# Attention and mixture of experts on one core: the first norm and the parts shared over more engines, and 16-bit parts for the scores

## The reference

```
h   = layernorm(x)                                  # over the 128 channels
s   = (h * w_lhs) @ (h * w_rhs).T                   # per sequence, 1024 x 1024
x   = x + softmax(s) @ h
g   = layernorm(x)
p   = softmax(g @ router_w.T)                       # 8 experts, the best two kept and made to sum to 1
x   = x + sum over the two experts of  p_e * (gelu(g @ w_fc[e] + b_fc[e]) @ w_proj[e] + b_proj[e])
```

## Time and profile before

| what | us |
|---|---|
| median of three runs (306.63 to 308.74) | 307.52 |
| the profiled execution | 307.93 |
| its span | 306.4 |
| PE busy, share of the span | 270.9, 88% |
| DVE busy | 236.1, 77% |
| ACT busy | 196.4, 64% |
| POOL busy | 180.6, 59% |

### The profile page before, as it was taken

One profiled execution on the slowest core, in us unless ns is written; L12 is line 12 of the kernel. 1 busy time (PEld: TensorE's weight loads), 2 busy tenths in 40 slices (PEclk: granted clock), 3 DMA queues, 4 the chain that ended last, 5 costly groups with the idle time before them and its releaser, 6 DMA issues.

```text
span 306.4 us, 8241 instructions
## 1 busy us (share of the span) xinstructions
PE 270.9 (88%) x2223; PEld 242.1 (79%) x2223; DVE 236.1 (77%) x1002; ACT 196.4 (64%) x427; POOL 180.6 (59%) x245
## 2 busy tenths in 40 slices
PE   7899999899989998899989499988999999999500
PEld 2479898788969887689879499978999999998500
DVE  4699898889878769988979988897665655676655
ACT  2447378896369772545776667675778887898300
POOL 8111036017577782787757857777777777766600
PEclk9999999999999999999999689999999999999955
DMA  6960000000401100111241152213333333221886
GB/s 195 415 282 4 0 3 0 3 0 0 143 26 56 45 18 20 37 44 37 79 136 45 37 136 88 72 46 108 106 92 95 100 97 90 80 64 46 318 283 272
DMA packets 15450, 28.51 MB, mean 93 GB/s; under 512 B 3904, under 2 KB 9920, under 8 KB 15152
## 3 DMA queue, kind: packets, MB, share of 16 engines
q1 hardware_dynamic: 10224, 16.88, 16.8%
q0 software_dynamic: 4608, 10.07, 9.9%
q10 hardware_dynamic: 576, 1.05, 1.0%
HBM read 15.83 MB, written 12.16 MB: 91 GB/s over the span
## 4 chain that ended last, share of the span: by engine, by line
PE 56%; DVE 26%; issue 5%; ACT 5%; POOL 3%; DMA 3%; DVEq 1%; SPq 0%; POOLq 0%; ACTq 0%
PE av_ps L1386 16%; PE av_ps L1181 14%; DVE neg_piece L1502 5%; PE sc_ps L1365 3%; PE sc_ps L1367 3%; PE sc_ps L1366 3%; DMA raw_proj<-results 2%; PE sc_ps L1170 2%; PE bank L1352 2%; DVE h_all L1844 2%; PE bank L1157 2%; PE bank L1159 1%; PE bank L1158 1%; ACT h_all L972 1%; PE sc_ps L1158 1%
## 5 line engine op out<-in xcount | busy, mean ns | idle before, releaser
L950 POOL DMA_INDIRECT results<-prob,result_row x71 | 68.7, 968 | 27.4 <-issue 10.4
L1094 ACT ACTIVATE raw_fc<-sc_ps,bfc,scale_down 128x128 f32<-128x128 f32 (+1 forms) x188 | 81.6, 530 | 0.8 <-PE sc_ps L1367 0.8
L1386 PE MATMUL av_ps<-raw_proj,raw_fc 128*128 x568 | 74.5, 283 | 5.9 <-DVE h_all L1844 5.7
L846 POOL DMA_INDIRECT slots<-stage,slot x64 | 63.8, 997 | 25.7 <-issue 18.9
L1386 PEld LDWEIGHTS av_ps<-raw_proj,raw_fc 128*128 128x128 f32 x568 | 68.6, 196 | 8.0 <-issue 7.6
L1181 PE MATMUL av_ps<-h_all,prob 128*128 128x137 f32 x512 | 73.2, 285 | 0.6 <-DVE lg_part L1533 0.5
L1181 PEld LDWEIGHTS av_ps<-h_all,prob 128*128 128x128 f32 x512 | 66.8, 190 | 4.4 <-DVE res L1530 1.6
L1365 PE MATMUL sc_ps<-h_all,wfc_hi 128*128 128x128 f16 (+1 forms) x188 | 43.5, 248 | 1.1 <-ACT raw_fc L1094 1.1
L1366 PE MATMUL sc_ps<-h_all,wfc_hi 128*128 128x128 f16 (+1 forms) x188 | 43.5, 248 | 0.0
L1367 PE MATMUL sc_ps<-h_all,wfc_lo 128*128 128x128 f16 (+1 forms) x188 | 43.4, 247 | 0.0
L1844 DVE TENSOR_TENSOR h_all<-av_ps,bpr 128x256 f32<-128x256 f32 (+1 forms) x47 | 16.9, 360 | 28.7 <-PE sc_ps L1367 24.8
(11 more groups left out here) (201 smaller groups left out, 524.5 us busy)
## 6 DMA issues: line engine op xcount, KB each, us to landing
slots_in<-slots SPq DMA_DIRECT2D x24, 132.0 KB
raw_fc<-in_w_fc_dram SPq DMA_DIRECT2D x1, 2048.0 KB, 10.9
raw_proj<-in_w_proj_dram SPq DMA_DIRECT2D x1, 2048.0 KB, 15.2
res<-in_x_dram SPq DMA_DIRECT2D x3, 512.0 KB, 5.8
slots_in<-slots SPq DMA_DIRECT2D x23, 66.0 KB
results<-prob,result_row POOLq DMA_INDIRECT x71, 2.3
slots<-raw_fc POOLq DMA_DIRECT2D x2, 528.0 KB, 4.1
slots<-stage,slot POOLq DMA_INDIRECT x64, 2.3
```

What stands on the lines that cost most here:

```text
L846: pool.indirect_dma_start(out=slots[:, :], out_offset=bass.IndirectOffsetOnAxis(ap=slot[:, n, k:k + 1], axis=0), in_=stage[:, b % 2, t, :] ...
L950: pool.indirect_dma_start(out=results[:, :], out_offset=bass.IndirectOffsetOnAxis(ap=result_row[a][:, h:h + 1], axis=0), in_=gated[a][h], ...
L1094: ins = act.activation(hid[:, a % NH, c, 0:halves_of(k) * P], up_ps(k, c), ACT.Gelu_apprx_tanh, bias=bfc[:, e, c:c + 1], scale=scale_down[ ...
L1386: mm = pe.matmul(o, hid[:, a % NH, c, rows], wpr[:, e, c, :], start=(c == 0 and h == 0), stop=(c == HC - 1), skip_group_check=True)
```

## The change

It does the following. The two w are loaded by ACT's queue, each also as a row for all partitions; DVE forms their product among the statistics of the second unit, finds its largest value, takes its power of two and scales the product with it (`scale_w`). The first norm also multiplies h by 2^12. The parts of h, q and the router weight become 16-bit floats; the exponent takes the factor that undoes the scaling from a column (`score_down`), and the gates take the router's (`rw_down`). POOL does the first unit's power ahead of its three selects. ACT and DVE share the first unit's tiles, POOL and DVE the second's. PE turns the first two units twice, into two banks each, and the low parts read the second copy; the first two blocks of scores wait for each part by itself. The router weight's parts are made later: POOL spreads the largest value by an all-reduce that stands behind its tiles (and ahead of the third unit's `scale`), DVE makes the scale after the fourth row maximum, ACT the high part and DVE the low part after the sixth. `stay_busy` is 16 and 2.

The diff, cut to its core (new buffers and semaphores and some lines of context are left out):

```diff
+H_UP = 2.0 ** 12
+RW_UP = 2.0 ** 13
...
-        hT_hi = sb("hT_hi", [P, 2, S], F32R)
-        hT_lo = sb("hT_lo", [P, 2, S], F32R)
-        q_hi = sb("q_hi", [P, 2, S], F32R)
-        q_lo = sb("q_lo", [P, 2, S], F32R)
+        hT_hi = sb("hT_hi", [P, 2, S], F16)
+        hT_lo = sb("hT_lo", [P, 2, S], F16)
+        q_hi = sb("q_hi", [P, 2, S], F16)
+        q_lo = sb("q_lo", [P, 2, S], F16)
...
-            return (second_h_made, t + 1) if u == 1 else (h_made, TU * (u - (u > 1)) + t + 1)
+            if u >= 2:
+                return h_made, 2 + TU * (u - 2) + t + 1
+            if t >= 2:
+                return second_h_made, 2 * u + t - 1
+            return (h_made, third_h_made)[u], t + 1
...
+        def second_turn(u):
+            return sc_ps[:, TU - 1 - u, :]
...
-            sp.dma_start(w_d[:, 0:1], w_lhs).then_inc(w_in, 16)
-            sp.dma_start(w_d[:, 1:2], w_rhs).then_inc(w_in, 16)
...
-            pool.memset(h_aug[:, :, :, D:D + 1], 1.0).then_inc(consts, 1)
...
+            pool.memset(h_aug[:, :, :, D:D + 1], H_UP).then_inc(consts, 1)
...
-            for u in range(4):
+            pool.wait_ge(consts, N_CONSTS - 3)
+            scale(0)
+            pool.affine_select(out=before[:, :], in_=ones16[:, :], compare_op=ALU.is_gt, fill=0.0,
+                               base=0, pattern=[[1, P]], channel_multiplier=-1).then_inc(consts, 1)
+            for m in (ident, ident16):
+                pool.affine_select(out=m[:, :], in_=m[:, :], compare_op=ALU.not_equal, fill=1.0,
+                                   base=0, pattern=[[-1, P]], channel_multiplier=1).then_inc(consts, 1)
+            scale(1)
+            pool.wait_ge(shift_made, 2)
+            for t in range(2):
+                pool.tensor_scalar(h_aug[:, 0, TU + t, 0:D], res[:, token_tile(1, t), :], rstd[:, 1, t:t + 1], shift[:, 1, t:t + 1],
+                                   ALU.mult, ALU.add).then_inc(third_h_made, 1)
+            pool.wait_ge(rwpeak_made, 1)
+            pool.partition_all_reduce(rw_peaks[:, :], rw_peak[:, :], P, RMAX).then_inc(rwpeaks_made, 1)
+            for u in range(2, 4):
                 scale(u)
...
-                act.activation(probT[:, m % RING, :], exp_source(n), ACT.Exp).then_inc(exp_made, 1)
+                act.activation(probT[:, m % RING, :], exp_source(n), ACT.Exp, scale=score_down[:, 0:1]).then_inc(exp_made, 1)
...
-            act.wait_ge(rw_in, 16)
-            act.activation(rw_hi, rwT[:, :], ACT.Copy).then_inc(rwhi_made, 1)
-            for t in range(TU):
+            for i, w in enumerate((w_lhs, w_rhs)):
+                act.dma_start(w_rows[:, i, :], w.rearrange("d o -> o d").to_broadcast([P, D])).then_inc(w_in, 16)
+                act.dma_start(w_d[:, i:i + 1], w).then_inc(w_in, 16)
+            for t in range(2):
...
+                if b == 0:
+                    act.wait_ge(rwup_made, 1)
+                    act.activation(rw_hi, rwT[:, :], ACT.Copy, scale=rw_up[:, 0:1]).then_inc(rwhi_made, 1)
...
-            stay_busy(20)
+            stay_busy(16)
...
+                if u < 2:
+                    for t in range(TU):
+                        mm = pe.transpose(second_turn(u)[:, t * P:(t + 1) * P], h_aug[:, 0, u * TU + t, 0:D], ident[:, :])
+                    mm.then_inc(h_turned_again, 1)
...
+                first = b == 0 and n < 2
+                if first:
+                    pe.wait_ge(hThi_made, c + 1)
+                    pe.wait_ge(qhi_made, 1)
+                if first and n == 1:
+                    pe.wait_ge(qlo_made, 1)
                 pe.matmul(o, q_hi[:, a, rows], hT_hi[:, a, cols], start=True, stop=False, skip_group_check=True)
+                if first:
+                    pe.wait_ge(hTlo_made, c + 1)
                 pe.matmul(o, q_hi[:, a, rows], hT_lo[:, a, cols], start=False, stop=False, skip_group_check=True)
+                if first:
+                    pe.wait_ge(qlo_made, 1)
                 mm = pe.matmul(o, q_lo[:, a, rows], hT_hi[:, a, cols], start=False, stop=True, skip_group_check=True)
...
             turn_h(0)
+            stay_busy(2)
             turn_h(1)
-            stay_busy(8)
             for b in range(B):
-                if b == 0:
-                    parts_made(0)
-                else:
+                if b >= 1:
                     pe.wait_ge(exp_made, exp_at(b - 1, 8))
                 score(b, 0)
-                if b == 0:
-                    parts_made(1)
-                else:
+                if b >= 1:
...
+                else:
+                    parts_made(1)
...
+            def take_stats(u, between=nothing):
                 if u < 2:
                     dve.wait_ge((x0_in, x_in[0])[u], 16)
                 else:
                     dve.wait_ge(x_in[u // 2], 16)
                 for t in range(TU):
                     ins = dve.bn_stats(stats[:, u % 2, t, :], res[:, token_tile(u, t), :])
+                    if t + 1 < TU:
+                        between()
                 ins.then_inc(stats_made, 1)
+                between()
                 dve.wait_ge(stats_made, u + 1)
...
-            def low_parts(u):
+            def low_hT(u):
                 dve.wait_ge(hThi_made, u + 1)
+                b = u // 2
+                cols = slice((u % 2) * HALF, (u % 2 + 1) * HALF)
+                src = second_turn(u) if u < 2 else bank[0][:, :]
+                if u < 2:
+                    dve.wait_ge(h_turned_again, u + 1)
+                else:
+                    dve.wait_ge(qhi_made, u + 1)
+                dve.tensor_tensor(hT_lo[:, b % 2, cols], src, hT_hi[:, b % 2, cols], ALU.subtract).then_inc(hTlo_made, 1)
+            def low_q(u):
                 dve.wait_ge(qhi_made, u + 1)
                 b = u // 2
                 cols = slice((u % 2) * HALF, (u % 2 + 1) * HALF)
-                src = bank[u % 2 if u < 2 else 0][:, :]
-                dve.tensor_tensor(hT_lo[:, b % 2, cols], src, hT_hi[:, b % 2, cols].bitcast(F32), ALU.subtract).then_inc(hTlo_made, 1)
-                dve.scalar_tensor_tensor(out=q_lo[:, b % 2, cols], in0=src, scalar=w_d[:, 2:3], in1=q_hi[:, b % 2, cols].bitcast(F32),
+                src = second_turn(u) if u < 2 else bank[0][:, :]
+                dve.scalar_tensor_tensor(out=q_lo[:, b % 2, cols], in0=src, scalar=w_d[:, 2:3], in1=q_hi[:, b % 2, cols],
                                          op0=ALU.mult, op1=ALU.subtract).then_inc(qlo_made, 1)
+            def low_parts(u):
+                low_hT(u)
+                low_q(u)
...
+            def scale_w():
+                dve.wait_ge(w_in, 64)
+                dve.tensor_tensor(w_rows[:, 2, :], w_rows[:, 0, :], w_rows[:, 1, :], ALU.mult).then_inc(w_chain, 1)
+                yield
+                dve.tensor_tensor(w_d[:, 2:3], w_d[:, 0:1], w_d[:, 1:2], ALU.mult).then_inc(w_chain, 1)
+                yield
+                dve.wait_ge(w_chain, 2)
+                dve.tensor_reduce(w_peak[:, :], w_rows[:, 2, :], AX_X, ALU.max, apply_absolute_value=True).then_inc(w_chain, 1)
+                yield
+                dve.wait_ge(w_chain, 3)
+                dve.tensor_scalar(w_peak[:, :], w_peak[:, :], 2.0 ** -100, 2.0 ** 126, ALU.max, ALU.min).then_inc(w_chain, 1)
+                yield
+                dve.wait_ge(w_chain, 4)
+                dve.tensor_scalar(w_pow2[:, :].bitcast(U32), w_peak[:, :].bitcast(U32), 0x7F800000, None, ALU.bitwise_and).then_inc(w_chain, 1)
+                yield
+                dve.wait_ge(w_chain, 5)
+                dve.reciprocal(w_up[:, :], w_pow2[:, :]).then_inc(w_chain, 1)
+                yield
+                dve.tensor_scalar(score_down[:, :], w_pow2[:, :], 2.0 * H_UP ** -2, None, ALU.mult).then_inc(w_chain, 1)
+                yield
+                dve.wait_ge(w_chain, 7)
+                dve.tensor_scalar(w_d[:, 2:3], w_d[:, 2:3], w_up[:, 0:1], 0.5, ALU.mult, ALU.mult).then_inc(w_made, 1)
+            def scale_rw():
+                dve.wait_ge(rwpeaks_made, 1)
+                dve.tensor_scalar(rw_peaks[:, :], rw_peaks[:, :], 2.0 ** -100, 2.0 ** 126, ALU.max, ALU.min).then_inc(rw_chain, 1)
+                dve.wait_ge(rw_chain, 1)
+                dve.tensor_scalar(rw_pow2[:, :].bitcast(U32), rw_peaks[:, :].bitcast(U32), 0x7F800000, None, ALU.bitwise_and).then_inc(rw_chain, 1)
+                dve.wait_ge(rw_chain, 2)
+                dve.reciprocal(rw_up[:, :], rw_pow2[:, :]).then_inc(rw_chain, 1)
+                dve.tensor_scalar(rw_down[:, :], rw_pow2[:, :], 1.0 / RW_UP, None, ALU.mult).then_inc(rw_chain, 1)
+                dve.wait_ge(rw_chain, 4)
+                dve.tensor_scalar(rw_up[:, :], rw_up[:, :], RW_UP, None, ALU.mult).then_inc(rwup_made, 1)
+            def low_rw():
+                dve.wait_ge(rwup_made, 1)
+                dve.wait_ge(rwhi_made, 1)
+                dve.scalar_tensor_tensor(out=rw_lo, in0=rwT[:, :], scalar=rw_up[:, 0:1], in1=rw_hi,
+                                         op0=ALU.mult, op1=ALU.subtract).then_inc(rwlo_made, 1)
...
```

(76 more changed lines are left out.)

## The result

The change makes the kernel slower: 311.93 us (median of 4 runs, 311.08 to 313.19) against 307.70 for the kernel before beside it; the ratio is 1.0141, 95% interval 1.0108 to 1.0173. The profiled execution took 311.44, of which 309.7 is its span (306.4 before). The forecast was 307.4 with a range to 310.9, so the time lies above the range, on the side of the rivals C and D, but not by their way. The shares of the chain of waits that ended last, to be held against the earlier trace rows: the DMAs and "issue" have grown by 3 points each.

A forecast was written before the change was run, and what follows sets the result against it. PE was over half the chain of waits, DVE a quarter; the first 20 us were latency, then DVE maxima. 307.93 + 1.9 (start) - 2.5 (16-bit matmuls) + 0.5 (exponent) = 307.8, against the median 307.4; range 303.9 to 310.9.

The forecast's parts named there:

- C: Slower: while DVE waits in the start, PE pauses 3.2 us and loses its clock, costing 2.0; 309.4 us, chance 0.15.
- D: Slower by more: the all-reduce's code load takes 2 us longer beside the weights' traffic, PE's clock falls; 311.4, chance 0.15.
- first account: The start, until the first batch's eighth row maximum ends: 21.2 against 19.30 before, so +1.9 us.
- statistics: In the start, DVE's work on w adds 1.15 us, second variance at 7.9; waiting for w's load taken as 0.
- two signs of a wrong start: Second maximum at 14.4 or later: start's steps wrong; eighth ending before 19.3 or after 23: whole forecast wrong.
- price of the all-reduce: In the start, POOL's code load takes 7.03 us, so DVE stands 2.25 ahead of the router's scale.
- scores' 0.015: In attention, each of 192 score matmuls gets 0.015 us shorter in 16 bits, starts 0.214 apart instead of 0.229.
- router's 0.06 a group: Router matmuls, limited by weight loads of now half the bytes, save 0.06 us in a group (bounds 0 and 0.2).
- second account: After the start, shorter 16-bit matmuls on PE give back 2.5 us (bounds -0.7 and -4.6).
- batch 1's first half: Matmuls there offer 0.8 us, but DVE's idle time is only 0.71, so 0.65 was counted.
- PE's wait for ACT behind batch 2's last maxima: In batch 2's second half PE already waits 0.99 us for ACT, so shorter matmuls gain 0 there.
- exponent's column: Reading the scale from a column costs ACT 0.08 us per exponent, +0.5 where ACT sets the pace (bounds 0 and 1.3).

## Why the prediction was wrong

**The first step that failed** is in the first account, statistics: "at half a microsecond an issue the last is there by 5.7 ... That is 0.4 at most, and I take 0." It took the landing time of w's column from a trace in which that column stood alone behind x, and applied it behind two loads of 128 times its size, on a second queue. The last column landed at 10.10, and x's first tiles 1.7 late. The row loads and the queue both lengthen the column's landing: without rows it took 3.1 on SP's queue and 5.3 on ACT's, with rows 5.7 and 7.9. I also priced the wait's place wrongly: the eight operations were costed, what stands behind a wait between them (second variance at 12.13 instead of 7.9) was not. PE's half clock in that pause, which no step had there, did most of the rest up to 18.95 for the second maximum (13.1 forecast): with dummy matmuls and the clock at 1.00 it started at 17.82. The two signs of a wrong start that I had named came with it, a second maximum after 14.4 and an eighth after 23.

**The second step that failed is the price of the all-reduce.** The mechanism was right, and its price too small: 8.63 from the end of POOL's tiles where w was early, not 7.03, and a pause of 4.37 for PE, with the clock gone. Had the first step held, the forecast of 307.4 would have been wrong by 3.6 all the same: the case that I gave 0.15 (D) was the one that comes, for a reason that stays open. In the changed kernel this whole term lies beside w's lateness, and it shows only as 0.08 of waiting. The Trainium skill (GPSIMD Engine Reference, Instruction dispatch) has about 6 us for the first call of freshly loaded code; the 5.92 here agrees, the 6.20 to 8.63 of the other runs are above it.

**The steps that held.** Without late w the second maximum came within 0.1 of the forecast. The scores' 0.015 became 0.013, the router's 0.06 a group became 0.07. The second account was -2.5: the 16-bit parts alone give -2.0. That it came so near is in part luck: batch 1's first half gave 1.0 where I had capped it at 0.65, and PE's wait for ACT behind batch 2's last maxima, which I put at nothing, takes 0.9 back. The exponent's column costs ACT 0.09 each as told, but nothing on the path that these runs can tell (304.51 beside 304.63), where I had +0.5. The ratios, 0.9906 and 0.9878, are too wide to exclude 0.5; in the profiles the stretch from the eighth maximum to the end of batch 2's takes 82.1 with the column and 82.0 without.

## What to carry to other kernels

Price a load that moves to another queue together with all that stands ahead of it and beside it, and ask what work stands behind the wait for it: a wait between two independent pieces of work delays both. Where two new delays lie side by side, taking one away shows little; fill the table of both before calling either harmless. A maximum over partitions of one column, in a latency-bound start, was cheap as a PE transpose of the broadcast column with a DVE reduction, and dear as POOL's all-reduce among POOL's own arithmetic.

## What the runs showed of the hardware that I had not expected

Loading 512 bytes into each of 128 partitions from the same 512 bytes of DRAM (64 KB) delayed what came behind it on its queue by microseconds: w's second column landed 5.7 after its issue behind two such loads on SP's queue and 3.1 without them, 7.9 and 5.3 on ACT's. Why is open. The Trainium skill (DMA: Bandwidth & Descriptors, Queues, rings and completion order) says that each DMA engine serves the queues in turn, packet by packet; the 5.3 for x's tiles beside ACT's four loads, 4.0 beside its two columns alone, and 3.1 without, fits that, though no run here shows the turns themselves.

The all-reduce's load took 5.92 to 8.63. The longest began early (9.99), the shortest at 14.57, both while the weights were loading at over 400 GB/s; and one that began at 9.92 took 7.06. So neither the traffic nor an early start alone explains the price, and its cause is open.

Keeping PE busy is worth only what the stretch is worth: 1.1 between two maxima where PE led, a loss of 2 where the fall of the clock was only moved to a place where it counts.
